# Which engine masks the narrow diagonal tiles: VectorE per head, or TensorE with one maximum over a bank

## The reference, cut to what matters

```python
attn = jnp.einsum('bqhd,bkhd->bhqk', Q, K) * scale
causal = jnp.tril(jnp.ones((S, S), dtype=bool))[None, None]
attn = jnp.where(causal, attn, NEG_INF)
attn = jax.nn.softmax(attn, axis=-1)
out = jnp.einsum('bhqk,bkhd->bqhd', attn, V).reshape(B, S, dim)
x = x + out @ w_proj + b_proj
h = layernorm(x)
real = h @ jnp.cos(theta + theta_noise)
imag = h @ jnp.sin(phi + phi_noise)
x = x + jnp.sqrt(real * real + imag * imag)
```

## Time and profile before

| | |
|---|---|
| median of three timed runs | 2019.36 us (2019.03 to 2027.15) |
| the profiled execution | 2022.42 us, of which the span of its instructions 2020.6 us |
| TensorE busy | 1971.6 us, 98% |
| VectorE busy | 1566.7 us, 78% |
| ScalarE busy | 1394.2 us, 69% |
| GpSimd busy | 861.3 us, 43% |

### The profile page before, as it was taken

How to read it: one execution, slowest core, us unless ns; L and a number is a source line. 1 busy time by engine, 2 the same in 40 slices (tenths; PEclk the granted TensorE clock), 3 DMA queues, 4 the chain that set the end, 5 groups by cost and what they waited for, 6 DMA issues and landing times.

```text
span 2020.6 us, 38150 instructions
## 1 busy us (share of the span) xinstructions
PE 1971.6 (98%) x12012; PEld 785.2 (39%) x12012; DVE 1566.7 (78%) x4101; ACT 1394.2 (69%) x2687; POOL 861.3 (43%) x1336
## 2 busy tenths in 40 slices
PE   7999999999999999999999999999999999989998
PEld 4333333334433344334343343434443343423334
DVE  4988888988778777797877868788687878677935
ACT  3357767786777676787777677677766777667774
POOL 3632426354443435543364453446434363451232
PEclk8899999999999999999999999999999999999999
DMA  6310212131111221221122111222111222130121
GB/s 134 81 44 13 74 57 73 56 92 57 58 59 55 69 71 59 76 86 62 60 70 70 64 59 54 74 71 90 57 57 60 69 75 75 36 111 7 49 94 63
DMA packets 130762, 133.30 MB, mean 66 GB/s; under 512 B 29434, under 2 KB 105722, under 8 KB 130554
## 3 DMA queue, kind: packets, MB, share of 16 engines
q1 hardware_dynamic: 127728, 128.29, 20.5%
q10 hardware_dynamic: 2832, 2.56, 0.6%
HBM read 38.49 MB, written 25.68 MB: 32 GB/s over the span
## 4 chain that ended last, share of the span: by engine, by line
PE 85%; ACT 4%; POOL 3%; issue 3%; DVE 3%; SPq 1%; DMA 1%; DVEq 0%; POOLq 0%; ACTq 0%
PE banks L1074 23%; PE banks L1059 22%; PE banks L1037 21%; PE banks L981 6%; PE banks L992 5%; PE banks L1019 3%; PE banks L926 2%; ACT probs L1178 2%; DVE chunk_max L1379 1%; SPq L739 1%; PE banks L915 1%; DVE banks L1374 1%; PE banks L908 1%; POOL guess L672 1%; PE banks L1045 1%
## 5 line engine op out<-in xcount | busy, mean ns | idle before, releaser
L1178 ACT ACTIVATE probs<-banks 128x512 f32<-128x512 f32 (+1 forms) x2240 | 1142.3, 598 | 350.8 <-PE banks L1059 311.1
L1379 DVE TENSOR_REDUCE chunk_max<-banks 128x1 f32<-128x512 f32 x1536 | 987.4, 684 | 230.2 <-PE banks L1037 228.1
L1037 PE MATMUL banks<-stack_k,stack_q 96*128 96x512 bf16 (+3 forms) x2560 | 689.2, 350 | 14.4 <-DVE chunk_max L1379 9.3
L1059 PE MATMUL banks<-stack_q,stack_k 99*128 99x512 bf16 (+3 forms) x2560 | 688.5, 350 | 6.1 <-ACT probs L1178 3.0
L1374 DVE CUSTOM_DVE_ANT_0 banks<-banks,row_mask 128x128 f32<-128x128 f32 (+3 forms) x1024 | 484.5, 509 | 113.7 <-PE banks L1037 112.5
L1074 PE MATMUL banks<-probs,v_one 128*17 128x512 f32 (+3 forms) x5120 | 543.3, 533 | 5.6 <-POOL probs L1506 4.9
L1059 PEld LDWEIGHTS banks<-stack_q,stack_k 99*128 99x128 bf16 x2560 | 227.0, 97 | 428.8 <-ACT probs L1178 225.4
L1037 PEld LDWEIGHTS banks<-stack_k,stack_q 96*128 96x128 bf16 x2560 | 233.6, 97 | 354.9 <-DVE chunk_max L1379 94.3
L1506 POOL TENSOR_SCALAR_AFFINE_SELECT probs<-probs 128x512 f32<-128x512 f32 x256 | 163.4, 646 | 251.0 <-ACT probs L1178 250.2
L1074 PEld LDWEIGHTS banks<-probs,v_one 128*17 128x17 f32 x5120 | 110.5, 96 | 273.4 <-ACT probs L1178 134.9
L646 POOL TENSOR_TENSOR turned<-raw,cos_t 128x512 f32<-128x512 f32 x62 | 78.7, 1270 | 236.1 <-ACT raw L1138 228.8
(11 more groups left out here) (158 smaller groups left out, 1153.7 us busy)
## 6 DMA issues: line engine op xcount, KB each, us to landing
stack_q<-parts SPq DMA_DIRECT2D x384, 64.0 KB, 2.6
stack_k<-parts SPq DMA_DIRECT2D x354, 64.0 KB, 2.6
sums<-o_raw SPq DMA_DIRECT2D x64, 256.0 KB, 2.2
rot<-raw SPq DMA_DIRECT2D x236, 64.0 KB, 2.0
xin<-x SPq DMA_DIRECT2D x16, 512.0 KB, 3.8
heads_t<-sums SPq DMA_DIRECT2D x26, 256.0 KB
mid<-x SPq DMA_DIRECT2D x13, 512.0 KB, 3.8
inverse<-inverses SPq DMA_DIRECT2D x26, 256.0 KB
```

Source lines behind the costliest of these rows:

```text
L1037: mm = nc.tensor.matmul(bank[:, n * wide:(n + 1) * wide], stack_q[u % 2][0:SPLIT_ROWS, t, h + n, j * P:(j + 1) * P], stack_k[u % 2][0:SPLI ...
L1059: mm = nc.tensor.matmul(bank[:, a * wide:(a + 1) * wide], stack_k[u % 2][0:ROWS, j // SUB, first + a, (j % SUB) * P:(j % SUB + 1) * P], st ...
L1178: nc.scalar.activation(probs[:, g % PROBS, first:first + many, w0:SPAN], bank, ACT.Exp).then_inc(s_exp, 1)
L1379: nc.vector.tensor_reduce(to, bank[:, 0:count * wide].rearrange("p (h n) -> p h n", h=count), AX.X, ALU.max).then_inc(s_emptied["DVE"], 1)
```

## The change

`MASKED_HEADS` goes from 4 to 1. In the two narrow diagonal tiles (four and two heads to a bank) TensorE now adds the mask with one more multiplication per head, and VectorE takes one plain maximum per bank. The tiles of one head per bank stay as they were. The planner's figure for these one-head tiles on VectorE goes from 0.13 to 0.17; the figures for the banks of several heads follow from `masks`: TensorE's grow by 0.06 per head, VectorE's fixed part is 0.07 in place of 0.13 per head.

```diff
-MASKED_HEADS = 4
+MASKED_HEADS = 1
@@ plan(), the maxima
                 job(name, "PE", 0.01 + wide / 2400 + (0.06 * n if d == tile // SUB and not masks(n) else 0.0), at + step * done / total - MAX_FIRST,
...
-                with_bank(name, name, "DVE", (0.13 if d == tile // SUB and masks(n) else 0.07 / n) * n + wide / 970, at + step * done / total)
+                with_bank(name, name, "DVE", (0.17 if d == tile // SUB and masks(n) else 0.07 / n) * n + wide / 970, at + step * done / total)
```

## The result

The changed kernel takes 2039.1 us (median of five, 2035.9 to 2041.36) against 2019.2 us, a ratio of 1.0089 with a 95% interval of 1.0068 to 1.0111: 0.9% slower. The profiled execution has a span of 2039.6 us against 2020.6.

A forecast was written before the change was run, and what follows sets the result against it. The prediction took TensorE to bound the kernel. Products, early relief and shorter waits summed as 27.3 - 2.0 - 3.9 = +21.4 us, which on 2019.36 gave 2040.8 us, 1.1% slower, range 2020 to 2054 us.

The forecast's parts named there:

- TensorE is the bound: Whole kernel: TensorE, busy 98% with some 1770 us of streaming in a 2020.6 us span, sets the time.
- Products, +27.3 us after 100 us, nothing before: Narrow diagonal tiles on TensorE: eight mask products per pair, 0.448 us, for 61 pairs add 27.3 us to the path.
- Relief, -5.9 us: TensorE's waits for VectorE: -2.0 us before 100 us, and -3.9 us from waits for masked maxima after.
- VectorE's time from start to start and not by duration: Narrow tiles on VectorE: 2.48 us per pair falls to 1.80, 43.5 us in all, not 139 by durations.
- Change of rows between products and maxima costs nothing; no mode change: TensorE between 128-row products and 96-row maxima: switching adds nothing, since products stay in the maxima's mode.
- The order, 0 with 8 us each way: Order of all engines' queues from `plan()`: taken as nothing, with 8 us each way for a tenth more or fewer excursions.
- The ceiling (1): TensorE's waits behind masked maxima are real stalls and all go, 24.2 us: 2020.5 us, no change; chance 0.11.
- VectorE setting the pace (2): VectorE, not TensorE, sets the pace through shared banks: -43.5 us, or -16.2 with products uncovered, 2003 us; chance 0.06.
- Rival 3: Mask products' weight loads on TensorE are not hidden, 0.097 us per product: +41.4 us, 2060.8 us; chance 0.08.
- Rival 4: `masks(count)` or the plan's items disagree with what is issued, so work stays as before: 2019 us; chance 0.01.

The follow-up runs named there:

- run 1: Kernel before with its own planned order, but mask products and plain maxima issued in the narrow tiles: ratio 1.0105 to the kernel before, span 2039.5 us.
- run 5: Kernel before with its order, each narrow-tile mask product issued twice while VectorE still masks: ratio 1.0236 to the kernel before, span 2069.6 us.
- run 3: Kernel before with its order, narrow-tile mask products issued once while VectorE still masks: ratio 1.0113 to the kernel before, span 2038.4 us.
- run 4: Kernel before with its order, plain maxima in the narrow tiles and no mask products: ratio 0.9986 to the kernel before, span 2015.4 us.
- run 6: Changed kernel with the planner's figure for one-head masked maxima kept at 0.13: ratio 1.0036 to the kernel before, span 2028.0 us.
- run 2: Changed kernel's order, but VectorE masks all tiles as before and no products are issued: ratio 1.0086 to the kernel before, span 2037.2 us.
- the table's third row: In the order planned for products in all tiles: span 2032.1 us with VectorE masking the narrow tiles, 2025.8 us with products there, difference -6.3 us.
- run 10: Order planned for products in all tiles, but products and plain maxima issued only in the narrow tiles: ratio 1.003 to the kernel before, span 2025.8 us.

## Why the prediction was right, by its steps

- **TensorE is the bound.** Held. Most of the streaming added is on the path: +20.8 us in run 1, 25 to 29 in run 5's second set.
- **Products, +27.3 us after 100 us, nothing before.** I had 61 pairs at 0.056 us a product. At the 0.059 measured these are 28.8 us; that all 512 come to 27.3 by their columns is a coincidence. What hides was mis-sized: 4 to 8 us went into stalls (run 3), where I had hidden 1.3. Net 19 to 23, about 21.
- **Relief, -5.9 us.** Too large by about half: -3 us by itself (run 4). On top of products it gives next to nothing in the order of before (+20.8 us with it in run 1, +21.0 without it in run 3, at equal clock). The sum came out at +20.8 against +21.4 because two errors cancel: products priced some 6 us too dear, and 3 to 6 us of relief that isn't there. That closeness is luck.
- **VectorE's time from start to start and not by duration.** Held: 37.6 us less busy time against 43.5 forecast and 139 by durations.
- **Change of rows between products and maxima costs nothing; no mode change.** Held: 0.06 us from each to the next in the rows above. The Trainium skill says that a change of tiling mode drains the engine (TensorEngine Tiling, "Key Properties"). The trace agrees around the values and the turning of a maximum (0.097 us in, 0.118 out) and shows no such cost between products and maxima.
- **The order, 0 with 8 us each way.** The value was right for this pair (2039.5 against 2039.6), and that is luck too, for the bound was wrong: 11.6 us between two orders with the same operations (run 6), 16.6 between those of run 2 and before (17.4 by the ratio). I named excursions as its price; they gave 9 us back, while the last stage took 8 and the wait at 1691 us 4.6. I had no term for a moved load that GpSimd waits on, though I named the queues.
- **Rivals.** The ceiling (1), 24.2 us, is not reached in the order of before: run 4 has 3. VectorE setting the pace (2) is false there. But by the table's third row, in an order made for products everywhere, masking the narrow tiles on VectorE costs more than the products do. How far it is VectorE there, and how far the empty room of products, is open (run 10). Rival 3 (loads not hidden) is excluded by 0.059 us. Rival 4 is excluded by the 512 records on L1035.

## What to carry to other kernels

Before adding to a bound engine's stream, add up its streaming from the starts of its instructions; what is left are stalls, some of which the first additions fill and a relief elsewhere may empty too, so look whether the two are the same before you add them. Take differences of a few us from many timed executions, or at equal granted clock, and not from two profiles. Where a planner makes the order from figures, an edit to a figure is an edit to the whole kernel: time the operations in the old order and the old operations in the new order before saying what either is worth. An order is made for its operations, and the price of an operation (+18.9, +2.4 or -6.3 us for the same swap in the narrow tiles) belongs to the pair.

## What the runs showed of the hardware

Eight bf16 multiplications of 128 columns, each with new weights and alternating between 128 and 96 rows, keep 0.058 or 0.059 us from start to start (the rows at 238.68 to 239.15), with the loads of 0.098 us hidden throughout. A masked maximum of 512 columns on VectorE with its accumulator read takes 0.607 us from start to start at the median and a plain one 0.598, though the records add up to 0.84 and 0.68. So mask and read together cost 0.009 us at full width. At 128 and 256 columns a head it is 0.248 and 0.38 us, and four or two of these for a bank against one of 0.598 are what the plain maximum saves. Into the values' 17-column mode TensorE takes 0.097 us over the streaming, out of it 0.118.
